# The last attention of a residual chain: four heads side by side on 32 rows each, and the softmax totals from exponentials added over the key tiles

## What is computed

```python
nx = _rmsnorm(X, g1)
Q = (nx @ Wq.T).reshape(B, S, H, dk).transpose(0, 2, 1, 3)   # B 2, S 512, H 4, dk 32
Kc = nx @ Wkc.T
Vc = nx @ Wvc.T
scores = jnp.einsum('bhsd,btd->bhst', Q, Kc) * scale
attn = jax.nn.softmax(scores, axis=-1)
out = jnp.einsum('bhst,btd->bhsd', attn, Vc)
out = out.transpose(0, 2, 1, 3).reshape(B, S, d) @ Wo.T
X = X + out
```

## Time and profile before

| | |
|---|---|
| median of three runs | 4737.11 us |
| the profiled execution, its own time | 4725.9 us |
| its span, first to last instruction | 4724.1 us |
| mean granted TensorE clock | 0.929 |
| TensorE busy | 88% of the span |
| the last attention | 4517.4 to 4643.6 us from the span's start |

### The profile page before, as it was taken

How to read it: one execution, slowest core, us unless ns; L and a number is a source line. 1 busy time by engine, 2 the same in 40 slices (tenths; PEclk the granted TensorE clock), 3 DMA queues, 4 the chain that set the end, 5 groups by cost and what they waited for, 6 DMA issues and landing times. The chain is left out here.

```text
span 4724.1 us, 82263 instructions
## 1 busy us (share of the span) xinstructions
PE 4135.0 (88%) x25322; PEld 2378.3 (50%) x25322; DVE 2861.7 (61%) x13564; ACT 2329.2 (49%) x6588; POOL 913.8 (19%) x4350
## 2 busy tenths in 40 slices
PE   6789999999999999999898999678888888888788
PEld 2247777777777777777732334222333323333223
DVE  4546666666666666666654444546666667666323
ACT  3335655555565556565533334224555544455433
POOL 0123333333333333333231000200011000000002
PEclk8889999999999999999999999768888888888889
DMA  0000000000000000000001000011112111211000
GB/s 9 24 7 2 2 2 2 2 2 2 2 2 2 2 2 2 2 2 2 20 16 46 0 1 1 29 59 43 53 46 64 54 60 52 64 45 44 14 17 5
DMA packets 48983, 94.51 MB, mean 20 GB/s; under 512 B 11440, under 2 KB 31936, under 8 KB 48288
## 3 DMA queue, kind: packets, MB, share of 16 engines
q1 hardware_dynamic: 48544, 89.24, 5.9%
HBM read 72.89 MB, written 15.39 MB: 19 GB/s over the span
## 5 line engine op out<-in xcount | busy, mean ns | idle before, releaser
L761 PE MATMUL ps<-g_h,w_p 128*128 128x128 f32 x4096 | 918.6, 306 | 0.0
L2138 ACT ACTIVATE t_ex<-ps 128x1024 f32<-128x1024 f32 (+1 forms) x480 | 471.9, 1021 | 570.8 <-PE ps L2085 557.1
L761 PEld LDWEIGHTS ps<-g_h,w_p 128*128 128x128 f32 x4096 | 618.0, 191 | 0.0
L757 PE MATMUL ps<-g_h,w_p 128*128 128x77 f32 x2048 | 456.7, 304 | 169.7 <-DVE g_h L829 141.0
L2233 DVE TENSOR_REDUCE t_ncol<-ps 128x1 f32<-128x512 f32 x768 | 486.6, 684 | 152.7 <-PE ps L2058 152.2
L825 DVE SCALAR_TENSOR_TENSOR g_used<-g_encg,g_e 128x77 f32<-128x77 f32 x3072 | 550.8, 230 | 0.0
L795 ACT ACTIVATE g_th<-ps 128x77 f32<-128x77 f32 x1024 | 241.4, 236 | 527.5 <-PE ps L757 527.5
L871 POOL TENSOR_SCALAR g_z<-g_tzr 128x1 f32<-128x1 f32 x1024 | 194.9, 190 | 1414.9 <-ACT g_tzr L804 1414.9
L757 PEld LDWEIGHTS ps<-g_h,w_p 128*128 128x128 f32 x2048 | 305.3, 188 | 305.8 <-DVE g_h L829 298.5
L776 PE MATMUL ps<-g_th,g_vrep 128*128 128x77 f32 x2048 | 456.7, 305 | 0.5 <-ACT g_th L795 0.5
L834 DVE TENSOR_REDUCE g_ntop<-ps 128x1 f32<-128x77 f32 x1024 | 244.6, 239 | 337.1 <-PE ps L776 336.3
(11 more groups left out here) (429 smaller groups left out, 6855.9 us busy)
## 6 DMA issues: line engine op xcount, KB each, us to landing
t_qst<-t_turn_q SPq DMA_DIRECT2D x288, 96.0 KB
t_kst<-t_turn_k SPq DMA_DIRECT2D x144, 96.0 KB
t_turn_q<-t_part SPq DMA_DIRECT2D x24, 384.0 KB, 2.5
t_turn_k<-t_part SPq DMA_DIRECT2D x12, 384.0 KB, 3.3
t_wf<-in_t_wf SPq DMA_DIRECT2D x6, 514.5 KB, 5.5
m_experts<-in_experts SPq DMA_DIRECT2D x1, 3072.0 KB, 13.2
t_wa<-in_t_wa SPq DMA_DIRECT2D x6, 448.0 KB, 3.3
t_wx<-in_t_wx SPq DMA_DIRECT2D x6, 448.0 KB, 4.2
```

Source lines behind the costliest of these rows:

```text
L757: M(att[c], w["att_h"], h[t % 2][:, c:c + 1].broadcast_to([P, S]), start=False, stop=True, skip_group_check=True).then_inc(*st.sem("att", c))
L761: return M(G[c][:, g], weights, h[t % 2][:, c:c + 1].broadcast_to([P, P]), start=False, stop=last, skip_group_check=True)
L2138: A(ex[0:kw, slot[pf, c, l, n]], ps[0:kw, at:at + 2], ACT.Exp, scale=SCALE).then_inc(*st.sem(f"{pf}e{n}", c))
```

## The change

A function of its own, `shared_attention`, takes the place of `attention` in `final_stage`.

- Its weights come with the pack `p7`, 416 columns more, the key's weights four times side by side, so that one product makes the key on all four groups of 32 rows.
- q stays as projected, head h on rows 32h to 32h + 31. For a tile, step a is four products, each on its 32 rows and into a bank of its own; two heads make a pair with two banks. VectorE takes the maximum of a pair at once, over 128 x 1024.
- The maxima are split into two bfloat16 parts, placed so that one group of four products (th) turns those of all heads into rows 32h and 32h + 1, copied once per batch. Step b is four products on 32 rows and then four bfloat16 products of two rows that add the shift. ScalarE's exponential goes over a pair, into a buffer that holds a whole batch.
- v is four products on 32 columns each, into bank 6. The totals no longer come from it: VectorE adds the exponentials of a batch over the four tiles (three adds for a pair), and four products with ones (tot) sum them into bank 7.
- Banks 0 to 5 go round as three pairs in the order of use (`uses`, `bank`, `readers`). A use waits for the reader of the one three before it.
- One pass each over a batch: logarithm, exponential, multiplication, output projection, residual add. Batch 1's maxima lie beside batch 0's attention; on ScalarE, batch 1's exponentials come after batch 0's inverse.

The new function and its call (bookkeeping and the removed function left out):

```diff
@@ -890,256 +890,209 @@
...
+def shared_attention(k, label, src, w):
     nc, ps = k.nc, k.ps
...
+    SCALE = 1.0 / math.sqrt(DK4)
+    PAIRS4 = H4 // 2
...
+        q, key = sb("q", [P, B, T]), sb("k", [P, B, T])
+        v = sb("v", [P, B, TT, DK4])
+        ncol, nb, row = sb("ncol", [P, B, TT, H4]), sb("nb", [P, B, TT, H4, DK4], BF16), sb("row", [P, B, T], BF16)
+        identb, onesb = sb("identb", [P, P], BF16), sb("onesb", [P, P], BF16)
+        ex = sb("ex", [P, TT, PAIRS4, 2, T])
+        inv, o = sb("inv", [P, B, T]), sb("o", [P, B, T])
+        added = sb("added", [P, B, PAIRS4, 2, T])
+        SUMS, TOTALS = 6, 7
+        order = [("a", 0, t) for t in range(TT)] + [("th", 0, 0)]
+        for t in range(TT):
+            order += [("b", 0, t), ("a", 1, t)] + ([("v", 0, t - 1)] if t else [])
+        order += [("v", 0, TT - 1), ("th", 1, 0), ("tot", 0, 0), ("b", 1, 0), ("w", 0, 0)]
+        for t in range(1, TT):
+            order += [("b", 1, t), ("v", 1, t - 1)]
+        order += [("v", 1, TT - 1), ("tot", 1, 0), ("w", 1, 0)]
+        two = [(t, p) for t in range(TT) for p in range(PAIRS4)]
...
+        uses = [("p", 0, 0, 0), ("p", 1, 0, 0), ("p", 2, 0, 0)]
+        for what, c, t in order:
+            if what in "ab":
+                uses += [(what, c, t, p) for p in range(PAIRS4)]
+            elif what in ("th", "w"):
+                uses.append((what, c, t, 0))
+        turn = {use: i for i, use in enumerate(uses)}
+        def bank(what, c, t=0, p=0):
+            return 2 * (turn[what, c, t, p] % 3)
+        def readers(what, c, t=0, p=0):
+            past, pc, pt, pp = uses[turn[what, c, t, p] - 3]
+            if past == "p":
+                return (("qc0", "kc0"), ("qc1", "kc1"), ("vc0", "vc1"))[pc]
+            return ({"a": f"m{pc}.{pt}.{pp}", "b": f"e{pc}.{pt}.{pp}", "th": f"rc{pc}", "w": f"res{pc}"}[past],)
+        filled = k.semaphore(f"{label}_filled")
...
+        def head(h):
+            return slice(DK4 * h, DK4 * h + DK4)
         @block.gpsimd
         def _(pool):
...
+            nc.gpsimd.memset(nb[:], 0.0).then_inc(filled, 1)
+            nc.gpsimd.memset(onesb[:], 1.0).then_inc(filled, 1)
+            nc.gpsimd.tensor_copy(identb[:], k.ident[:]).then_inc(filled, 1)
+            pool.wait_ge(filled, 3)
         @block.tensor
         def _(pe):
             M = nc.tensor.matmul
...
+            for c in range(B):
+                M(ps[:, 2 * c], w["wq"], src[:, c], start=True, stop=True).then_inc(*st.sem(f"q{c}"))
+                M(ps[:, 2 * c + 1], w["wk"], src[:, c], start=True, stop=True).then_inc(*st.sem(f"k{c}"))
+                for t in range(TT):
+                    mm = M(ps[:, 4 + c, t * DK4:(t + 1) * DK4], src[:, c, t * P:(t + 1) * P], w["wv"], start=True, stop=True)
+                mm.then_inc(*st.sem(f"v{c}"))
+            pe.wait_ge(filled, 3)
+            for what, c, t in order:
+                if what in ("a", "b"):
+                    if what == "a" and t == 0:
+                        pe.wait_ge(*st.at(f"qc{c}"))
+                        pe.wait_ge(*st.at(f"kc{c}"))
+                    elif what == "b" and t == 0:
+                        pe.wait_ge(*st.at(f"rc{c}"))
+                    tile = slice(t * P, (t + 1) * P)
+                    for p in range(PAIRS4):
+                        for reader in readers(what, c, t, p):
+                            pe.wait_ge(*st.at(reader))
+                        for i in range(2):
+                            d, at = head(2 * p + i), bank(what, c, t, p) + i
+                            if what == "a":
+                                mm = M(ps[:, at], q[d, c, tile], key[d, c], start=True, stop=True)
+                            else:
+                                M(ps[:, at], key[d, c, tile], q[d, c], start=True, stop=False)
+                        if what == "a":
+                            mm.then_inc(*st.sem(f"a{c}.{t}.{p}"))
+                    if what == "b":
+                        for p in range(PAIRS4):
+                            for i in range(2):
+                                d, at = slice(DK4 * (2 * p + i), DK4 * (2 * p + i) + 2), bank(what, c, t, p) + i
+                                mm = M(ps[:, at], onesb[d], row[d, c], start=False, stop=True, tile_position=(DK4 * (2 * p + i), 0))
+                            mm.then_inc(*st.sem(f"b{c}.{t}.{p}"))
+                elif what == "th":
+                    pe.wait_ge(*st.at(f"lo{c}"))
+                    for reader in readers(what, c):
+                        pe.wait_ge(*st.at(reader))
+                    for j in range(TT):
+                        mm = M(ps[:, bank(what, c), j * P:(j + 1) * P], nb[:, c, j].rearrange("p h n -> p (h n)"), identb[:],
+                               start=True, stop=True)
+                    mm.then_inc(*st.sem(f"th{c}.0"))
+                elif what == "v":
+                    if t == 0:
+                        pe.wait_ge(*st.at(f"vc{c}"))
+                        if c:
+                            pe.wait_ge(*st.at(f"o{c - 1}"))
+                    for p in range(PAIRS4):
+                        pe.wait_ge(*st.at(f"e{c}.{t}.{p}"))
+                        for i in range(2):
+                            mm = M(ps[head(2 * p + i), SUMS], v[:, c, t], ex[:, t, p, i], start=(t == 0), stop=(t == TT - 1),
+                                   skip_group_check=True)
+                    mm.then_inc(*st.sem(f"v{c}.{t}"))
+                elif what == "tot":
+                    pe.wait_ge(*st.at(f"ad{c}.{TT - 1}.{PAIRS4 - 1}"))
+                    if c:
+                        pe.wait_ge(*st.at(f"ln{c - 1}"))
+                    for h in range(H4):
+                        mm = M(ps[head(h), TOTALS], k.ones[:, 0:DK4], added[:, c, h // 2, h % 2], start=True, stop=True, skip_group_check=True)
+                    mm.then_inc(*st.sem(f"tot{c}.0"))
+                else:
+                    pe.wait_ge(*st.at(f"o{c}"))
+                    for reader in readers(what, c):
+                        pe.wait_ge(*st.at(reader))
+                    M(ps[:, bank(what, c)], w["wo"], o[:, c], start=True, stop=True).then_inc(*st.sem(f"w{c}.0"))
         @block.scalar
         def _(act):
...
+            A = nc.scalar.activation
+            for c in range(B):
+                act.wait_ge(*st.at(f"q{c}"))
+                A(q[:, c], ps[:, 2 * c], ACT.Copy).then_inc(*st.sem(f"qc{c}"))
+            for c in range(B):
+                for t, p in two:
+                    act.wait_ge(*st.at(f"b{c}.{t}.{p}"))
+                    if c:
+                        act.wait_ge(*st.at(f"v{c - 1}.{t}"))
+                        act.wait_ge(*st.at(f"ad{c - 1}.{max(t, 1)}.{p}"))
+                    at = bank("b", c, t, p)
+                    A(ex[:, t, p], ps[:, at:at + 2], ACT.Exp, scale=SCALE).then_inc(*st.sem(f"e{c}.{t}.{p}"))
+                act.wait_ge(*st.at(f"tot{c}.0"))
+                A(inv[:, c], ps[:, TOTALS], ACT.Ln).then_inc(*st.sem(f"ln{c}"))
+                act.wait_ge(*st.at(f"ln{c}"))
+                A(inv[:, c], inv[:, c], ACT.Exp, scale=-1.0).then_inc(*st.sem(f"inv{c}"))
         @block.vector
         def _(dve):
             V = nc.vector
...
+            def add(c, t, p):
+                dve.wait_ge(*st.at(f"e{c}.{t}.{p}"))
+                if t > 1:
+                    dve.wait_ge(*st.at(f"ad{c}.{t - 1}.{p}"))
+                V.tensor_tensor(added[:, c, p], ex[:, 0, p] if t == 1 else added[:, c, p], ex[:, t, p], ALU.add)\
+                    .then_inc(*st.sem(f"ad{c}.{t}.{p}"))
+            def maxima(c):
+                for t, p in two:
+                    dve.wait_ge(*st.at(f"a{c}.{t}.{p}"))
+                    at = bank("a", c, t, p)
+                    V.tensor_reduce(ncol[:, c, t, 2 * p:2 * p + 2], ps[:, at:at + 2], AX, ALU.max, negate=True)\
+                        .then_inc(*st.sem(f"m{c}.{t}.{p}"))
+                    if c and t:
+                        add(0, t, p)
+                if c == 0:
+                    dve.wait_ge(filled, 1)
+                dve.wait_ge(*st.at(f"m{c}.{TT - 1}.{PAIRS4 - 1}"))
+                V.tensor_copy(nb[:, c, :, :, 0], ncol[:, c]).then_inc(*st.sem(f"hi{c}"))
+                dve.wait_ge(*st.at(f"hi{c}"))
+                V.tensor_tensor(nb[:, c, :, :, 1], ncol[:, c], nb[:, c, :, :, 0], ALU.subtract).then_inc(*st.sem(f"lo{c}"))
+                dve.wait_ge(*st.at(f"th{c}.0"))
+                V.tensor_copy(row[:, c], ps[:, bank("th", c)]).then_inc(*st.sem(f"rc{c}"))
+            for c in range(B):
+                dve.wait_ge(*st.at(f"k{c}"))
+                V.tensor_copy(key[:, c], ps[:, 2 * c + 1]).then_inc(*st.sem(f"kc{c}"))
+                dve.wait_ge(*st.at(f"v{c}"))
+                V.tensor_copy(v[:, c].rearrange("p t n -> p (t n)"), ps[:, 4 + c, 0:P]).then_inc(*st.sem(f"vc{c}"))
+            for c in range(B):
+                maxima(c)
+            for c in range(B):
+                if c:
+                    for t, p in two:
```

(63 more changed lines are left out.)

178 lines of the change are left out of this document (removed).

## The result

The changed kernel takes 4676.49 us (median of four runs, of which three took 4675.11 to 4677.3, with 4675.68 as their own median, and the fourth, disturbed, 5374.83 at a mean granted clock of 0.631) where the kernel before took 4736.73 (4736.12 to 4740.1): a ratio of 0.987 with a 95% interval of 0.9851 to 0.989, 60.2 us less. The forecast was 4677.

A forecast was written before the change was run, and what follows sets the result against it. TensorE's float32 products were taken to bound the last attention (126.2 us), wholly on the path. Stage -65.9, load +1.0 and clock +4.5 sum to -60.4 us: 4676.7 on the median, range 4662 to 4702.

The forecast's parts named there:

- What bounds, and what a saved microsecond is worth: Last attention, 126.2 us: TensorE-busy, no overlap with neighbours, so a microsecond off the stage is one off the kernel.
- Start: Last attention's opening: first scores at S + 7.7 us instead of S + 12.8, S being the stage's start; projections kept at 7.7.
- Maxima, shift row: Batch 0's maxima, VectorE slower at 1.14 us a pair, end at S + 18.0; shift row, 1.7 us, at S + 19.7.
- Middle part: Batch 0's attention beside batch 1's maxima: VectorE is the bound, 4.56 us a tile; ends at S + 39.5.
- Batch 0's end and batch 1: Batch 1's exponentials start about S + 43.0; its attention takes 8.9 us: first step 3.5, then two tiles of 2.7.
- Tail: Stage's end, from batch 1's last exponentials through totals and projection to residual add: 8.4 us, ending at S + 60.3.
- The clock: Slower granted clock after TensorE's two holes, where VectorE finishes and splits maxima: +4.5 us, between 0 and 18.
- Load: Weight pack ahead of the final norm grows from 13 KB to about 226 KB: +1.0 us, between 0.5 and 1.5.
- (a): Rival, score products: only two row groups run at once; +8 us, 4685; chance 0.12.
- (b): Rival, score products: heads of 32 rows run one after another; +30 us, 4707; chance 0.06.
- (d): Rival, stage's products: weights no longer loaded ahead when row group changes; 1.24 us each, 30 us slower, 4767; chance 0.03.
- (c): Rival, new stage: clock stays at 1.2 GHz; +18 us instead of 4.5, 4690 to 4695; chance 0.11.

The follow-up runs named there:

- after: The changed kernel's first profile, no further edit: median 4676.49 us, ratio 0.987 to the kernel before; stage 65.6 us.
- b2: The changed kernel again, no edit, five rounds on one chip with b1: 4658.62 us, ratio 0.9871 to the kernel before.
- e4: Changed kernel plus ten unread 128-row products (norm ahead, before both shift rows, before last output projection): 4650.37 us, ratio 0.9866; stage 57.2 us.
- b1: The kernel of e4 a second time, beside b2 on one chip: 4656.2 us, ratio 0.9866; stage 57.2 us.
- e6: The kernel of e2 with each score product on all 128 rows, still one after another: 4708.38 us, stage 96.0 us.
- e3: Changed kernel with score and shift products on two row groups, heads 0 and 1 computed twice: 4696.94 us, stage 84.1 us.
- e2: Changed kernel with all four heads' score and shift products on rows 0 to 31: 4748.56 us, stage 154.0 us.
- e7: Kernel before the change, its score products cut to 64 of 128 rows, values unchanged: 4753.07 us, stage 148.9 us against 126.2.
- e1: Kernel before the change, run again with no edit: median 4728.36 us of ten runs, ratio 1.0008; stage 126.2 us.

## Why the prediction was right, step by step

**What bounds, and what a saved microsecond is worth.** Right. The stage has the same hard edges in after, and nothing in it is hidden: 60.6 us off the stage, less 2.0 given back around it, stand against 60.2 off the median. That 4676.7 was forecast and 4676.49 measured is luck to that degree: the same kernel took 4658.62 in b2, and the ratio's interval leaves room for 52 to 71 us.

**Start.** Forecast S + 7.7, measured 9.6, and 5.4 in e4. This step was mis-sized. I kept the 7.7 us that the projections took before, without asking at which clock: the whole stretch was granted 0.75, and its first product took 2.08 us, which takes 1.10 at a clock of 1.00 (e4). What made it 2.3 us too long is seen by halves: batch 0's projections took 4.55 us at 0.62, batch 1's 3.10 at 1.00 (4524.90 to 4528.00), and e4's 2.7 a batch. So some 1.5 us of it were clock and 0.8 slower steps, and none of it is in the +4.5, which I had put down for the holes alone. In after the clock is lower still (0.54), behind a norm whose products are few; with three more of them in that norm it is 1.00 (e4).

**Maxima, shift row.** Forecast 10.3 and 1.7 us, measured 10.3 and 2.0; in e4 10.3 and 1.7. VectorE's pace of 1.14 from the earlier trace rows carried over to the hundredth (9.14 us for eight).

**Middle part.** Forecast 19.8, measured 22.3, in e4 20.1. Bound and pace as forecast, VectorE without a hole from the second tile on. The 2.5 us more are the first tile at half clock: the first transposed scores take 2.09 us instead of 1.14, and VectorE waits 4.31 us for its first maximum of batch 1 where e4's waits 2.31.

**Batch 0's end and batch 1.** Forecast 3.5 and 8.9, measured 4.2 and 7.9, in e4 3.2 and 8.0. I had given the first step of batch 1 3.5 us for the handing round of banks; it took 3.2 (4575.30 to 4578.48), and the tile steps took 2.47 and 2.28 instead of 2.7. Tail: forecast 8.4, measured 9.2, in e4 8.5; the difference is the last projection at half clock, 1.82 us instead of 1.13.

**The clock.** Forecast +4.5, between 0 and 18; measured 65.6 - 57.2 = 8.4 in the stage. The two holes that I named are there, TensorE idle for 2.84 and 2.15 us ahead of the shift rows, and half clock follows both; the projections, and the last output projection after 2.10 us of idleness, are two more places, which I had not named. Step by step, after less e4: 3.4 us go with the two holes (0.2 in the shift row, 2.2 in the middle part, 1.0 in the step behind it), where I had 4.5, and 5.0 with the places not named (4.3 in the projections, 0.7 in the last output projection). Without the +4.5 my working gives 60.3 and e4 gives 57.2. So the forecast of 64.8 was close to 65.6 by luck, since two errors cancelled: 3.1 us too much in the steps (2.3 at the start, 1.0 in batch 1), 3.9 too little for the clock.

**Load.** Forecast +1.0, measured +0.8 at the first product that waits for it. What stands behind the stage took 1.0 us more, which I had at nothing; e4 and b1 have 80.0 and 80.1 there, so the clock at the stage's end is its likely cause.

**Rivals.** (a) is out for the changed kernel: eight passes of four heads have their successor 0.97 us on, not 1.9. (b) is out; its price of +30 met e6's 96.0, partly by luck, as said there. (d) is out: 0.24 us a product in those eight passes. (c) came true in part: 0.85 to 0.88 over the long stretches and not 0.5 to 0.7, 8.4 us and not 18.

The weak point, had the heads not overlapped, would have been the prices of (a) and (b). I took them from full clock, +8 and +30; in single runs they are +18.5 and +88 (e3, e2). My forecast of 4707 for (b) would have met 4748.56, a kernel slower than before. What I lacked is that the granted clock can go with the rows.

Against four row groups at once stood 3.07 times the speed of one, in the Trainium skill ("TensorE: Matmul & The Clock Gate", Part 3, Measured speedup vs the span model). Here, at a clock of 1.00 in both, eight passes take 3.63 us one after another on 128 rows (e6) and 0.97 four at a time (after): 3.7 times. The measurement decides.

## What to carry to other kernels

Small heads side by side in row groups pay twice on this chip: they overlap, and together they fill all 128 rows, where the same products one after another on 32 rows, or two at a time on 64 in the middle part, ran at 1.2 GHz. When a stage is shortened this way the next bound is the vector work, and the waits of TensorE for it cost more than their length, since the products behind them run at half clock; ten idle products gave back 8 of 65 us of the stage, about half of that by the three ahead of it. And a duration carried over from a profile must be read together with the granted clock of its stretch.

## What the runs showed of the hardware that I had not expected

- The granted clock went with how many rows the products fill, and not with TensorE's busy time alone. At a TensorE busy in 96 to 100% of 40 us: 128 rows in use 1.00 (e6), two groups of 32 at once 0.52 (e3), 32 rows 0.50 (e2). Only e2 and e6 differ in nothing but the rows and the values computed. In e2 the clock fell in mid-stream; in e3 it fell at a hole and stayed down, though 64 rows had run at 1.00 in the maxima before. With two of three products on 64 rows it moved between 0.51 and 1.00 (e7). Why, and from how many rows on, these runs do not show.
- The Trainium skill says, in the table of "TensorE: Matmul & The Clock Gate" under Why this matters for your kernels, that a single product of 32 rows takes the time of one of 128. At equal clock the passes here bear that out (0.87 us at half clock in e2, 0.45 at full clock in e6); but a stream of such products lost the clock with which this holds, 6.99 us for eight passes against 3.63.
- Four row groups of float32 products overlap almost fully, with what follows 0.97 us after eight passes at a pass of 0.43: 0.1 us beyond the stream, where I had put 0.2.
- Ten executions of one kernel spread over 27 us (e1). The two profiles of it at hand differ by 16.1 us ahead of the stage, while the stage and what follows it are the same to 0.1 us.
